# Recommendation model on one core: in the last step, the first half's second top layer placed behind the second half's Gram products

## The chip, the core and the metric

The kernel runs on one core of a Trainium2 chip. The metric is the device time of one execution in microseconds (us), the median of several runs. TensorE multiplies matrices, VectorE and ScalarE move and transform data, GpSimd issues the gathers of table rows, SyncE issues the plain transfers. In the profile they are called PE (PEld for its weight loads), DVE, ACT, POOL and SP.

## The reference

For 2048 samples the model runs a small net on 13 dense features, gathers 26 table rows of 64 numbers, forms all pairwise products of the 27 vectors, and runs a second net on them:

```
x = relu(dense @ Wb0 + bb0)            # 13 -> 512
x = relu(x @ Wb1 + bb1)                # -> 256
d = relu(x @ Wb2 + bb2)                # -> 64
sp = emb[arange(26)[None, :], sparse_idx]          # 2048 x 26 x 64, tables of 12500 rows
T = concatenate([sp, d[:, None, :]], axis=1)       # 27 vectors a sample
Z = einsum('bnd,bmd->bnm', T, T)                   # Gram products
h = concatenate([d, Z[:, lower triangle]], axis=1) # 64 + 351
h = relu(h @ Wt0 + bt0)                # -> 512
h = relu(h @ Wt1 + bt1)                # -> 256
p = sigmoid(h @ Wt2 + bt2)             # -> 1
```

## The kernel before, in words

The 2048 samples are taken in 8 steps of 256. A step gathers 52 pieces of 128 rows (26 tables, two halves of 128 samples), one indirect transfer each, issued by GpSimd (L260). All engines run their own programs, written out by hand in a fixed order, and wait for each other by semaphores; nothing is scheduled by a compiler. So the order on an engine is the order in which the code issues.

In the first seven steps TensorE works on the top net of the step before while rows of this step land. The last step (`last_step`, L477 for TensorE) is written differently: its gathers bring the first half's 26 pieces first, then the second half's, so that the first half can be finished while the second half still lands. For each half `h`:

- `turn_last(h, r)` (L334) transposes the rows of run `r` of tables (four tables a run, two in the last, r = 6) when they have landed; VectorE or ScalarE copies them out of PSUM (`spread_last`, L688 and L550).
- `gram_last(h)` (L373) forms the Gram products: 128 small matmuls, which the profile shows as 256 passes, since each f32 matmul of this kernel is two passes, a weight load and a matmul each. It waits for all copies of its half.
- VectorE transposes the products in two pieces (`turn_gram`, L693 and L695), ScalarE packs them (`pack`, L568), TensorE transposes three tiles (`turn_feat`, L383), ScalarE moves them (L574).
- `top_0` (L394 and L400) is the first top layer in four blocks of 128 outputs: a block is one matmul on the dense part (`top_0_d`) and three on the pairs. ScalarE and VectorE apply relu (L580, L701).
- the second top layer is one matmul that adds the bias (`top_1_bias`, L421) and four on the hidden layer (`top_1_sum`, L431). `top_1` is both in a row.
- `logit` (L706) is VectorE's product with the last weights; it reads the PSUM tile `ps_t1` of the second layer. The bias matmul of the second half waits for the first half's logit, since it overwrites that tile.

After the last logit come one sigmoid on ScalarE and the transfer of the result (L235). The code of the last step, of all three engines, is straight: no loop.

Of the kernel before, what the change touches and what calls it, by code (L numbers as in the profile page):

```python
# [91 lines left out]
def build(nc, x, idx, emb, wb0, bb0, wb1, bb1, wb2, bb2, wt0, wt1, bt1, wt2, bt2, out):  # L92
    emb_rows = emb.rearrange("t v d -> (t v) d")

    with ExitStack() as ctx:  # L95
# [100 lines left out]
        def top_0_blocks(u, side):  # L196


            if side == 0:
                return ps_t0[:, 0:2 * P].rearrange("p (m c) -> p m c", m=2)  # L200
            return ps_feat[u][:, 0:2, :]
# [10 lines left out]
        def unit_products(n):  # L212

            return ps_gram[:, :, 0:HALF * VECS].rearrange("p b (c v) -> p v b c", v=VECS)[:, 0:n]

        def turned_half(h, r):

            first, n = RUNS[r]
            part = slice(DIM * h, DIM * (h + 1))
            return (vecs_st[part, :, first:first + n].rearrange("p c t -> p t c"),  # L220
                    ps_turn[(h * NR + r) % 2][part, 0:n, :])
# [61 lines left out]
        def _(pe):  # L283
# [39 lines left out]
            def turn_last(h, r):  # L323

                first, n = RUNS[r]
                k = h * NR + r
                pe.wait_ge(rows_landed_last[h][r], 16 * n)
                if k >= 2 and k % 2 == 0:
                    pe.wait_ge(vecs_act, (STEPS - 1) * ACT_RUNS + k // 2)
                if k >= 2 and k % 2 == 1:  # L330
                    pe.wait_ge(vecs_dve, (STEPS - 1) * DVE_RUNS + k // 2)
                cols = DIM * (h + 1)
                for j in range(n):
                    turned = nc.tensor.transpose(ps_turn[k % 2][0:cols, j, :], rows[:, first + j, 0:cols], ident[:, :])  # L334
                turned.then_inc(rows_turned, 1)
# [21 lines left out]
            def gram_last(h):  # L357

                i = STEPS - 1

                pe.wait_ge(vecs_act, i * ACT_RUNS + (NR * (h + 1) + 1) // 2)
                pe.wait_ge(vecs_dve, i * DVE_RUNS + NR * (h + 1) // 2)
                if h == 0:
                    pe.wait_ge(d_placed, STEPS)
                else:

                    pe.wait_ge(gram_turned, i * 4 + 2)
                part = slice(DIM * h, DIM * (h + 1))
                for u in range(2):
                    for g in range(HALF):  # L370
                        for v in range(4):
                            c = 64 * u + 16 * v + g
                            summed = nc.tensor.matmul(  # L373
                                ps_gram[32 * v:32 * v + 32, u, g * VECS:(g + 1) * VECS],
                                vecs_st[part, c, :], vecs_st[part, c, 0:VECS],
                                start=True, stop=True, tile_position=(DIM * h, 32 * v))
                summed.then_inc(gram_summed, 1)

            def turn_feat(i, u):

                pe.wait_ge(feat_packed, i * 2 + u + 1)
                for k in range(PAIR_TILES):
                    turned = nc.tensor.transpose(ps_feat[u][0:PAIR_ROWS, k, :],  # L383
                                                 feat[:, u, k * PAIR_ROWS:(k + 1) * PAIR_ROWS], ident[:, :])
                turned.then_inc(feat_turned, 1)

            def top_0_d(i, u, m):

                if m == 0 and u == 0:
                    pe.wait_ge(d_copied, i + 1)  # L390
                if m == 0 and u == 1:

                    pe.wait_ge(t0_act, i * 2 + 1)
                nc.tensor.matmul(top_0_blocks(u, m // 2)[:, m % 2, :], wt0_sb[0:D_ROWS, PAIR_TILES, m * P:(m + 1) * P],  # L394
                                 d_t[:, u, :], start=True, stop=False)
# [10 lines left out]
            def top_0(i, u, blocks=range(T0 // P), begun=False):  # L406

                for m in blocks:
                    if m > 0 or not begun:
                        top_0_d(i, u, m)  # L410
                    if m == 0:

                        pe.wait_ge(feat_act, i * 2 + u + 1)
                    top_0_pairs(i, u, m)

            def top_1_bias(i, u):

                if u == 1:

                    pe.wait_ge(logit_ready, i * 2 + 1)  # L420
                nc.tensor.matmul(ps_t1[:, 0:T1], ones[0:1, :], bt1_sb[:, :], start=True, stop=False)  # L421

            def top_1_sum(i, u):

                for k in range(T0 // P):
                    if k == 0:

                        pe.wait_ge(t0_act, i * 2 + u + 1)
                    if k == 2:
                        pe.wait_ge(t0_dve, i * 2 + u + 1)  # L430
                    summed = nc.tensor.matmul(ps_t1[:, 0:T1], ht0_t[:, k, :], wt1_sb[:, k, :],  # L431
                                              start=False, stop=(k == T0 // P - 1))
                summed.then_inc(t1_summed, 1)
# [22 lines left out]
            def land(i, turn_run):  # L456

                turn_run(0)
                top_0(i - 1, 0)
                turn_run(1)  # L460
                turn_run(2)
                top_1(i - 1, 0)
                top_0(i - 1, 1)
                turn_run(3)
                turn_run(4)
                top_1(i - 1, 1)
                turn_run(5)
                turn_run(6)
# [8 lines left out]
            def last_step():  # L477
                i = STEPS - 1
                land(i, lambda r: turn_last(0, r))
                gram_last(0)  # L480
                turn_last(1, 0)
                turn_feat(i, 0)
                for r in range(1, NR - 3):
                    turn_last(1, r)

                top_0(i, 0, blocks=range(0, 2))
                turn_last(1, NR - 3)
                top_0(i, 0, blocks=range(2, 4))
                top_1_bias(i, 0)
                turn_last(1, NR - 2)  # L490
                top_1_sum(i, 0)
                turn_last(1, NR - 1)
                gram_last(1)

                top_0_d(i, 1, 0)
                top_1_bias(i, 1)
                turn_feat(i, 1)
                top_0(i, 1, begun=True)
                top_1_sum(i, 1)

            pe.wait_ge(bottom_loaded, 16 * BOTTOM_LOADS)
            bottom_0(0)
# [153 lines left out]
        def _(dve):  # L656
# [29 lines left out]
            def spread_last(h, r):  # L686
                dve.wait_ge(rows_turned, (STEPS + h) * NR + r + 1)
                nc.vector.tensor_copy(*turned_half(h, r)).then_inc(vecs_dve, 1)  # L688

            def turn_gram(i, u):  # L690

                dve.wait_ge(gram_summed, i * 2 + u + 1)
                nc.vector.transpose(gram_s[u][:, 0:VECS * SLOTS], unit_products(VECS)).then_inc(gram_turned, 1)  # L693

                nc.vector.transpose(gram_s[u][:, VECS * SLOTS:WRAP * SLOTS], unit_products(DELTAS))\  # L695
                    .then_inc(gram_turned, 1)

            def relu_top(i, u):

                dve.wait_ge(t0_summed, i * 4 + 2 * u + 2)  # L700
                nc.vector.tensor_scalar(ht0_t[:, 2:4, :], top_0_blocks(u, 1), 0.0, None, ALU.max).then_inc(t0_dve, 1)  # L701

            def logit(i, u):

                dve.wait_ge(t1_summed, i * 2 + u + 1)
                nc.vector.scalar_tensor_tensor(out=ht1_w[:, :], in0=ps_t1[:, 0:T1], scalar=0.0, in1=wt2_sb[:, :],  # L706
                                               op0=ALU.max, op1=ALU.mult,
                                               accum_out=logits[:, bass.ds(i * 2 + u, 1)]).then_inc(logit_ready, 1)
# [4 lines left out]
            def land(i, spread_run, head=None):  # L713
                spread_run(1)
                relu_top(i - 1, 0)
                logit(i - 1, 0)
                spread_run(3)
                if head:
                    head()
                relu_top(i - 1, 1)  # L720
                logit(i - 1, 1)
                spread_run(5)
# [18 lines left out]
            def last_step():  # L741
                i = STEPS - 1
                land(i, lambda r: spread_last(0, r))
                turn_gram(i, 0)
                spread_last(1, 0)
                spread_last(1, 2)
                spread_last(1, 4)
                relu_top(i, 0)
                spread_last(1, 6)
                logit(i, 0)  # L750
                turn_gram(i, 1)
                relu_top(i, 1)
                logit(i, 1)

# [79 lines left out]
```

## Time and profile before

| | |
|---|---|
| time, median of 3 runs | 552.0 us (551.23 to 552.62) |
| span of the profiled execution, first to last instruction | 551.0 us |
| TensorE busy (matmul) | 310.5 us, 56% |
| GpSimd busy | 394.4 us, 72% |
| VectorE, ScalarE busy | 127.8 us and 134.6 us |
| mean granted TensorE clock | 0.703 of full speed |

The profiled execution has no time of its own beside its span; the span is 1.0 us below the median of the runs. The chain of waits, followed back from the last instruction, names at each point what the end depended on. A timeline row gives the start, the busy time, the engine, the line, what is written and read, the count, and in brackets the idle time ahead and what ended it. A windows row gives for a stretch the busy time of each engine with its instructions, and the granted clock, where 1.00 is 2.4 GHz and 0.50 is 1.2 GHz.

### The profile page before, as it was taken

The numbers are of one execution on the slowest core, as the hardware profiler recorded it, in microseconds if no ns is written. First come the engines' busy times: TensorE is split into PE (matmuls) and PEld (weight loads), VectorE is DVE, ScalarE is ACT, GpSimd is POOL, SyncE is SP. The second block draws the span as 40 slices with busy tenths as digits, with TensorE's granted clock in tenths as the row PEclk, the third lists the DMA queues.
The fourth block names the chain that finished last, engine by engine and source line by source line (L and its number), as shares of the span: only waits on it lengthen the run. The fifth ranks groups of instructions, "written<-read, shape, count | busy, mean of one in ns | idle before, by whom it ended". The sixth has DMA issues, their size and how long they took to land.

```text
span 551.0 us, 8032 instructions
## 1 busy us (share of the span) xinstructions
PE 310.5 (56%) x3370; PEld 226.6 (41%) x3370; DVE 127.8 (23%) x190; ACT 134.6 (24%) x197; POOL 394.4 (72%) x422
## 2 busy tenths in 40 slices
PE   4799966825556327164373455552463742775566
PEld 1333325713445217152272334441253522664546
DVE  5213232222220222220212202302222112221110
ACT  1124333502242213122152021420133221311101
POOL 5777777777777777777777777777777777777710
PEclk9996796776586566675576765766667756795686
DMA  7233323333243322333233332343323432333310
GB/s 204 25 27 28 26 27 28 28 26 27 29 26 27 26 27 26 27 26 26 26 26 26 26 27 26 27 26 27 28 25 26 26 26 27 26 27 28 28 10 2
DMA packets 16181, 16.53 MB, mean 30 GB/s; under 512 B 7691, under 2 KB 8972, under 8 KB 16153
## 3 DMA queue, kind: packets, MB, share of 16 engines
q0 software_dynamic: 13312, 13.66, 31.7%
q1 hardware_dynamic: 2170, 2.41, 1.4%
q10 hardware_dynamic: 684, 0.24, 0.2%
q8 instruction: 12, 0.20, 0.1%
q14 instruction: 3, 0.02, 0.0%
HBM read 16.28 MB, written 0.01 MB: 30 GB/s over the span
## 4 chain that ended last, share of the span: by engine, by line
POOL 68%; issue 24%; PE 4%; DMA 2%; DVE 1%; POOLq 1%; ACT 1%; DVEq 0%; ACTq 0%
POOL rows L260 68%; DMA rows<-in_emb,idx_step 1%; PE ps_t L431 1%; DMA idx_raw<-in_idx 1%; PE ps_gram L351 1%; PE ps_t L400 1%; PE ps_gram L373 0%; PE ps_feat L400 0%; PE ps_turn L334 0%; ACT vecs_mv L545 0%; POOLq L95 0%; DVE gram_s L693 0%; DVE gram_s L695 0%; PE ps_feat L383 0%; PE ps_feat L394 0%
## 5 line engine op out<-in xcount | busy, mean ns | idle before, releaser
L260 POOL DMA_INDIRECT rows<-in_emb,idx_step x416 | 392.7, 944 | 130.8 <-issue 130.5
L320 PE MATMUL ps_turn<-ident,rows 128*128 128x128 f32 x182 | 41.0, 365 | 167.3 <-DMA rows<-in_emb,idx_step 162.1
L320 PEld LDWEIGHTS ps_turn<-ident,rows 128*128 128x128 f32 x182 | 26.2, 181 | 183.6 <-issue 174.3
L545 ACT ACTIVATE vecs_st<-ps_turn 128x512 f32<-128x512 f32 (+1 forms) x28 | 25.9, 926 | 215.2 <-PE ps_turn L320 215.0
L351 PE MATMUL ps_gram<-vecs_mv,vecs_st 128*32 128x54 f32 x1792 | 43.5, 296 | 25.2 <-ACT vecs_mv L545 13.3
L545 ACT ACTIVATE vecs_mv<-ps_turn 64x512 f32<-64x512 f32 (+1 forms) x56 | 54.0, 964 | 0.3
L351 PEld LDWEIGHTS ps_gram<-vecs_mv,vecs_st 128*32 128x32 f32 x1792 | 40.8, 173 | 29.3 <-issue 13.8
L431 PE MATMUL ps_t<-wt_sb,ht_t 128*128 128x256 f32 x128 | 52.0, 578 | 0.0
L683 DVE COPY vecs_st<-ps_turn 128x512 f32<-128x512 f32 x21 | 21.3, 1014 | 120.5 <-PE ps_turn L320 120.5
L683 DVE COPY vecs_mv<-ps_turn 64x512 f32<-64x512 f32 x42 | 43.7, 1042 | 0.3
L431 PEld LDWEIGHTS ps_t<-wt_sb,ht_t 128*128 128x128 f32 x128 | 36.4, 298 | 15.4 <-issue 8.2
L706 DVE SCALAR_TENSOR_TENSOR ht_w<-ps_t,wt_sb 128x256 f32<-128x256 f32 x16 | 6.8, 424 | 136.6 <-PE ps_t L431 136.6
L693 DVE STREAM_TRANSPOSE gram_s<-ps_gram 128x864 f32<-128x864 f32 x16 | 17.3, 1083 | 82.1 <-PE ps_gram L351 67.7
L400 PE MATMUL ps_t<-feat_t,wt_sb 117*128 117x128 f32 x192 | 34.3, 328 | 0.6 <-ACT feat_t L574 0.6
L297 PE MATMUL ps_t<-hb,wb_sb 128*128 128x512 f32 x64 | 31.7, 653 | 3.3 <-DVE hb L668 3.3
L400 PEld LDWEIGHTS ps_t<-feat_t,wt_sb 117*128 117x128 f32 x192 | 31.2, 240 | 0.9 <-ACT feat_t L574 0.9
L400 PE MATMUL ps_feat<-feat_t,wt_sb 117*128 117x128 f32 x192 | 29.7, 296 | 0.0
L400 PEld LDWEIGHTS ps_feat<-feat_t,wt_sb 117*128 117x128 f32 x192 | 27.4, 215 | 0.0
L568 ACT ACTIVATE feat<-gram_s 128x351 f32<-128x351 f32 x16 | 13.4, 840 | 56.0 <-DVE gram_s L695 56.0
L297 PEld LDWEIGHTS ps_t<-hb,wb_sb 128*128 128x128 f32 x64 | 13.4, 216 | 21.1 <-issue 16.3
L383 PE MATMUL ps_feat<-ident,feat 128*117 128x128 f32 x48 | 12.5, 383 | 14.5 <-ACT feat L568 14.5
L421 PE MATMUL ps_t<-bt_sb,ones 1*128 1x256 f32 x32 | 17.3, 637 | 0.0
(52 smaller groups left out, 235.8 us busy)
## 6 DMA issues: line engine op xcount, KB each, us to landing
rows<-in_emb,idx_step POOLq DMA_INDIRECT x416, 3.4
wt_sb<-in_wt SPq DMA_DIRECT2D x1, 1024.0 KB
wb_sb<-in_wb SPq DMA_DIRECT2D x1, 512.0 KB
wt_sb<-in_wt SPq DMA_DIRECT2D x1, 512.0 KB
idx_raw<-in_idx SPq DMA_DIRECT2D x1, 208.0 KB, 3.9
wt_sb<-in_wt ACTq DMA_DIRECT2D x1, 128.0 KB
x_t<-in_x ACTq DMA_DIRECT2D x1, 104.0 KB
wb_sb<-in_wb SPq DMA_DIRECT2D x1, 64.0 KB
```

The source lines that it names most:

```text
L260: nc.gpsimd.indirect_dma_start(rows[:, t, h * DIM:(h + 1) * DIM], None, emb_rows, bass.IndirectOffsetOnAxis(idx_step[:, c:c + 1], 0)).then ...
L297: summed = nc.tensor.matmul((ps_t0, ps_t1)[m][:, :], wb1_sb[:, k, m * P:(m + 1) * P], hb0[:, k, :], start=(k == 0), stop=(k == B0 // P - 1))
L320: turned = nc.tensor.transpose(ps_turn[r % 2][:, j, :], rows[:, first + j, :], ident[:, :])
L351: summed = nc.tensor.matmul(ps_gram[32 * v:32 * v + 32, b, g * 2 * VECS:(g + 1) * 2 * VECS], vecs_st[:, c, :], vecs_mv[:, c, :, :].rearran ...
L383: turned = nc.tensor.transpose(ps_feat[u][0:PAIR_ROWS, k, :], feat[:, u, k * PAIR_ROWS:(k + 1) * PAIR_ROWS], ident[:, :])
L400: summed = nc.tensor.matmul(top_0_blocks(u, m // 2)[:, m % 2, :], wt0_sb[0:PAIR_ROWS, k, m * P:(m + 1) * P], feat_t[:, u, k, :], start=Fal ...
L421: nc.tensor.matmul(ps_t1[:, 0:T1], ones[0:1, :], bt1_sb[:, :], start=True, stop=False)
L431: summed = nc.tensor.matmul(ps_t1[:, 0:T1], ht0_t[:, k, :], wt1_sb[:, k, :], start=False, stop=(k == T0 // P - 1))
L545: moved = nc.scalar.activation(to, source, ACT.Copy)
L568: nc.scalar.activation(feat[:, u, :].rearrange("p (e i) -> p e i", e=DELTAS), bass.AP(gram_s[u], SLOTS, [[WRAP * SLOTS, P], [SLOTS, DELTAS ...
L683: moved = nc.vector.tensor_copy(to, source)
L693: nc.vector.transpose(gram_s[u][:, 0:VECS * SLOTS], unit_products(VECS)).then_inc(gram_turned, 1)
```

## The change

On TensorE the bias matmul and the four summing matmuls of the first half's second top layer no longer stand around the transposes of run 5 of the second half, but behind all of the second half's Gram products and ahead of `top_0_d` of the second half. The second half's bias matmul moves from ahead of `turn_feat` to directly ahead of its sum, since both layers are now issued by the unsplit `top_1`. On VectorE the first half's logit moves behind the two transposes of the second half's Gram products. The number of instructions is the same, and ScalarE, GpSimd and SyncE issue what they issued.

```diff
@@ -486,17 +486,15 @@
                 top_0(i, 0, blocks=range(0, 2))
                 turn_last(1, NR - 3)
                 top_0(i, 0, blocks=range(2, 4))
-                top_1_bias(i, 0)
                 turn_last(1, NR - 2)
-                top_1_sum(i, 0)
                 turn_last(1, NR - 1)
                 gram_last(1)
 
+                top_1(i, 0)
                 top_0_d(i, 1, 0)
-                top_1_bias(i, 1)
                 turn_feat(i, 1)
                 top_0(i, 1, begun=True)
-                top_1_sum(i, 1)
+                top_1(i, 1)
 
@@ -747,8 +745,8 @@
                 spread_last(1, 4)
                 relu_top(i, 0)
                 spread_last(1, 6)
+                turn_gram(i, 1)
                 logit(i, 0)
-                turn_gram(i, 1)
                 relu_top(i, 1)
                 logit(i, 1)
```

TensorE before, from the last block of the first half's `top_0` to the second half's `top_0_d` (`ps_turn` takes transposed rows, `ps_gram` Gram products, `ps_t` the top layers):

```order
L421 MATMUL ps_t<-bt_sb,ones 128x256
L334 MATMUL ps_turn<-ident,rows 128x128 [waits vecs_act,rows_landed_last1_5]
L334 MATMUL ps_turn<-ident,rows 128x128 x3
L431 MATMUL ps_t<-wt_sb,ht_t 128x256 [waits t0_act]
L431 MATMUL ps_t<-wt_sb,ht_t 128x256
L431 MATMUL ps_t<-wt_sb,ht_t 128x256 [waits t0_dve]
L431 MATMUL ps_t<-wt_sb,ht_t 128x256
L334 MATMUL ps_turn<-ident,rows 128x128 [waits vecs_dve,rows_landed_last1_6]
L334 MATMUL ps_turn<-ident,rows 128x128
L373 MATMUL ps_gram<-vecs_st 32x27 [waits gram_turned,vecs_dve,vecs_act]
L373 MATMUL ps_gram<-vecs_st 32x27 x127
L394 MATMUL ps_t<-d_t,wt_sb 128x128 [waits t0_act]
```

TensorE now, the same stretch:

```order
L334 MATMUL ps_turn<-ident,rows 128x128 [waits vecs_act,rows_landed_last1_5]
L334 MATMUL ps_turn<-ident,rows 128x128 x3
L334 MATMUL ps_turn<-ident,rows 128x128 [waits vecs_dve,rows_landed_last1_6]
L334 MATMUL ps_turn<-ident,rows 128x128
L373 MATMUL ps_gram<-vecs_st 32x27 [waits gram_turned,vecs_dve,vecs_act]
L373 MATMUL ps_gram<-vecs_st 32x27 x127
L421 MATMUL ps_t<-bt_sb,ones 128x256
L431 MATMUL ps_t<-wt_sb,ht_t 128x256 [waits t0_act]
L431 MATMUL ps_t<-wt_sb,ht_t 128x256
L431 MATMUL ps_t<-wt_sb,ht_t 128x256 [waits t0_dve]
L431 MATMUL ps_t<-wt_sb,ht_t 128x256
L394 MATMUL ps_t<-d_t,wt_sb 128x128 [waits t0_act]
```

Five matmuls, ten passes, left the space between the landing rows and now follow the Gram products. VectorE before, at the end of its program (`ht_w` is written by the logit, `gram_s` takes the transposed products):

```order
L688 COPY vecs_st<-ps_turn 64x2x128 [waits rows_turned]
L706 SCALAR_TENSOR_TENSOR ht_w,logits<-ps_t,wt_sb 128x256 [waits t1_summed]
L693 STREAM_TRANSPOSE gram_s<-ps_gram 128x864 [waits gram_summed]
L695 STREAM_TRANSPOSE gram_s<-ps_gram 128x416
L701 TENSOR_SCALAR ht_t<-ps_feat 128x256 [waits t0_summed]
L706 SCALAR_TENSOR_TENSOR ht_w,logits<-ps_t,wt_sb 128x256 [waits t1_summed]
```

VectorE now, the same place (the changed kernel is two lines shorter above it, so its line numbers are lower by two):

```order
L686 COPY vecs_st<-ps_turn 64x2x128 [waits rows_turned]
L691 STREAM_TRANSPOSE gram_s<-ps_gram 128x864 [waits gram_summed]
L693 STREAM_TRANSPOSE gram_s<-ps_gram 128x416
L704 SCALAR_TENSOR_TENSOR ht_w,logits<-ps_t,wt_sb 128x256 [waits t1_summed]
L699 TENSOR_SCALAR ht_t<-ps_feat 128x256 [waits t0_summed]
L704 SCALAR_TENSOR_TENSOR ht_w,logits<-ps_t,wt_sb 128x256 [waits t1_summed]
```

The first logit and the two transposes have changed places; nothing else moved on VectorE.

## Rows read from the trace of the kernel before

**Rows 1.** The page: span, and the chain by engine.

```profile
span 551.0 us, 8032 instructions
...
POOL 68%; issue 24%; PE 4%; DMA 2%; DVE 1%; POOLq 1%; ACT 1%; DVEq 0%; ACTq 0%
```

**Rows 2.** The chain's end in order of time: start us, us, what.

```profile
522.43 3.35 DMA rows<-in_emb,idx_step
...
532.45 2.37 issue
...
548.36 0.42 DVE ht_w L706
```

**Rows 3.** Timeline of GpSimd: the last gather.

```profile
524.93 0.95 POOL L260 DMA_INDIRECT rows<-in_emb,idx_step  x1 [0.30 <-issue]
```

**Rows 4.** Timeline of TensorE's matmuls, from 526 us to the end.

```profile
526.65 3.24 PE L431 MATMUL ps_t<-wt_sb,ht_t 128*128 128x256 f32 x8
529.72 0.38 PE L334 MATMUL ps_turn<-ident,rows 128*128 128x128 f32 x2
530.83 1.62 PE L373 MATMUL ps_gram<-vecs_st 64*32 64x27 f32 x170 [0.73 <-issue]
534.82 0.93 PE L373 MATMUL ps_gram<-vecs_st 64*32 64x27 f32 x86 [2.37 <-issue]
535.68 0.49 PE L394 MATMUL ps_t<-d_t,wt_sb 65*128 65x128 f32 x2
536.10 1.16 PE L421 MATMUL ps_t<-bt_sb,ones 1*128 1x256 f32 x2
538.29 0.99 PE L383 MATMUL ps_feat<-ident,feat 128*117 128x128 f32 x3 [1.03 <-ACT feat L568]
539.86 1.65 PE L400 MATMUL ps_t<-feat_t,wt_sb 117*128 117x128 f32 x6 [0.58 <-ACT feat_t L574]
...
546.42 1.91 PE L431 MATMUL ps_t<-wt_sb,ht_t 128*128 128x256 f32 x8
```

**Rows 5.** Timeline of VectorE around the first half's logit.

```profile
530.14 0.59 DVE L688 COPY vecs_st<-ps_turn 64x256 f32<-64x256 f32 x1 [6.47 <-PE ps_turn L334]
530.76 0.42 DVE L706 SCALAR_TENSOR_TENSOR ht_w<-ps_t,wt_sb 128x256 f32<-128x256 f32 x1
```

**Rows 6.** Windows: us, busy us (instructions) by engine, PEclk, DMA share, GB/s.

```profile
525.95:529.30 3.35, 3.35 (x11) 2.81 (x12) 0.00 (x0) 1.03 (x1) 0.00 (x0) 0.50 0.16 10
529.40:532.70 3.30, 2.33 (x175) 1.91 (x173) 1.02 (x3) 0.00 (x0) 0.00 (x0) 1.00 0.02 5
532.80:536.10 3.30, 1.28 (x89) 1.13 (x89) 0.30 (x1) 0.00 (x0) 0.00 (x0) 1.00 0.02 5
536.20:539.50 3.30, 2.05 (x5) 1.02 (x5) 1.18 (x2) 1.01 (x2) 0.00 (x0) 0.50 0.00 0
...
543.00:546.40 3.40, 3.40 (x17) 3.40 (x17) 0.00 (x0) 0.38 (x1) 0.00 (x0) 0.50 0.02 5
546.50:549.00 2.50, 1.82 (x9) 1.25 (x8) 0.85 (x3) 0.13 (x1) 0.00 (x0) 1.00 0.00 0
```

**Rows 7.** Timeline of TensorE's matmuls from 486 to 505 us.

```profile
486.24 0.39 PE L394 MATMUL ps_feat<-d_t,wt_sb 65*128 65x128 f32 x2
...
487.13 0.39 PE L394 MATMUL ps_feat<-d_t,wt_sb 65*128 65x128 f32 x2
...
489.62 1.99 PE L431 MATMUL ps_t<-wt_sb,ht_t 128*128 128x256 f32 x8
...
495.81 0.64 PE L334 MATMUL ps_turn<-ident,rows 128*64 128x128 f32 x2 [1.89 <-DMA rows<-in_emb,idx_step]
497.12 1.85 PE L373 MATMUL ps_gram<-vecs_st 64*32 64x27 f32 x117 [0.68 <-ACT vecs_st L550]
500.36 2.14 PE L373 MATMUL ps_gram<-vecs_st 64*32 64x27 f32 x128 [1.39 <-issue]
504.37 0.41 PE L373 MATMUL ps_gram<-vecs_st 64*32 64x27 f32 x11 [1.87 <-issue]
```

**Rows 8.** Windows of an earlier stretch, columns as in rows 6.

```profile
488.50:492.00 3.50, 3.11 (x16) 2.02 (x13) 1.62 (x3) 1.33 (x3) 2.66 (x3) 1.00 0.34 26
496.50:505.00 8.50, 4.63 (x258) 4.28 (x259) 0.18 (x1) 0.57 (x1) 6.37 (x8) 0.50 0.31 31
```

## The prediction

> **What bounds the kernel.** I read the chain by engine first: GpSimd holds 68% of it, with gathers issued one after another [rows 1]. The change touches nothing ahead of 523 us, so only the end counts. The chain's end shows where GpSimd hands over: a gather begun at 522.43 lands 3.35 us later [rows 2], and the last one begins at 524.93 [rows 3]. From there TensorE's timeline is nearly the whole chain: the first half's second layer (526.65), the transposes of run 6 (529.72), the Gram products (530.83, resumed at 534.82), the turning of the pair features (538.29), the first top layer (539.86), the second (546.42) [rows 4]. Then the windows are read for the clock: half speed from 525.95, full from 529.4 to 536.1, half from 536.2 to 546.4, full at the end [rows 6]. So an edit here has three prices: its passes, the wait it hides in, and what it does to the clock.
>
> **Step 1, the Gram products start earlier.** The last gather, at the same 3.35 us, lands at 524.93 + 3.35 = 528.28. Run 6 was turned only at 529.72, because the eight passes at 526.65 stood ahead of it on TensorE. Without them it starts at 528.3. From that turn to the first Gram pass it took 1.11 us (530.83 - 529.72), in which VectorE's 0.59 us copy lies [rows 5]. A turn after an idle TensorE costs 0.64 us instead of 0.38 [rows 7, 4], so 1.11 to 1.37 us. The Gram products begin at 529.4 to 529.7: 1.2 us earlier. The ends: where the eight passes run at full speed (1.99 us, [rows 7, 8]) they would be over by about 528.5 before too, and the gain is 0.2; at most it is 1.4. The bias matmul ahead of run 5 lay in a wait for rows and was free. The first logit began at 530.76 [rows 5], after the copy and beside the Gram products: moving it gains nothing.
>
> **Step 2, the Gram products themselves.** Before they took 530.83 to 535.75, 4.9 us, with a pause of 2.37 us after 170 passes in which TensorE waits for nothing shown [rows 2, 4]. The first half's Gram products pause as well, after 117 and after 245 passes, that is 128 apart [rows 7]: the pause goes by the position in the instruction stream. Ten passes fewer stand ahead now, so I expect it after 180 passes instead of 170, with 76 behind it. In full clock nothing changes in the sum: passes ahead and behind add up to 256 as before, 4.9 us. In half clock a pass takes 2.14/128 = 16.7 ns, and from one resumption to the next, 128 passes and a pause, 504.37 - 500.36 = 4.0 us [rows 7]. Counting 52 passes, one such stretch, and 76 passes: 0.9 + 4.0 + 1.3 = 6.2 us, 1.2 more. Which clock? Before, the full speed at 529.4 came after a stretch of 3.35 us with TensorE busy in all of it [rows 6], and the eight passes were most of that. They are gone; from about 526.9 to 528.3 TensorE now idles. I take half speed, +1.2 us (bounds 0 and 1.3). That cancels step 1: the products end at about 535.75, as before.
>
> The Trainium skill, "Runtime: NRT & Kernel Launch", section "Instruction fetch mechanics", says that instructions come in blocks of 256 and that the cost of crossing a block is mostly hidden. The count agrees with the 128 passes of two instructions between pauses; "mostly hidden" does not, at 1.39, 1.87 and 2.37 us [rows 7, 4]. By that rule the Gram products would take 2.4 us less before and after alike, and the difference would stay.
>
> **Step 3, the moved layer where it now stands.** From the last Gram pass (535.75) to the turning of the features (538.29) there are 2.5 us, VectorE's transposes and ScalarE's packing, in which TensorE had only the dense part and the second half's bias. Now stand there, with 0.4 us for the dense part (535.68 to 536.10) and the first layer's ten passes: at half clock 3.1 us for eight (526.65 to 529.72) and 0.8 for the bias at the same price a pass, together 4.3 us, 1.8 more than the cover; at full clock 1.8 to 1.9 for eight (546.42), 0.5 and 0.2, together 2.6, 0.1 more [rows 4, 7]. Behind it wait `turn_feat` and with it ScalarE's move and all of `top_0`. The clock rises somewhere in this run, I think near its end: +1.3 us (bounds 0.1 and 1.8). The logit on VectorE then comes at about 540, seven microseconds before its next customer: free.
>
> **Step 4, the first top layer of the second half.** Its 30 passes took 539.86 to 546.42, 6.6 us, at half clock [rows 4, 6]. In full clock a block of eight takes 487.13 - 486.24 = 0.89 us [rows 7], so 30 take 3.3. Before, TensorE had idled ahead of it, and the clock rose only 6.6 us into the unbroken run. The rise at 529.4 came about 3.5 us into one that began at 525.82. Now TensorE is in unbroken work from the resumed Gram products, near 534.5, to about 540; with 3.5 to 6.6 us the rise falls at 538.0 to 541.1. Then comes about 1 us of waiting for ScalarE's move. Once up, the clock held through windows with 2.33 and 1.28 of 3.30 us busy and fell after the second [rows 6]; so it probably holds for a good part of `top_0`. I take two thirds of it in full clock: -2.1 us (bounds 0 and -3.3).
>
> The Trainium skill, "TensorE: Matmul & The Clock Gate", section "What's actually happening", says the monitor is free-running and does not start with the kernel. No row here shows the phase of another execution; by that rule step 4 differs from run to run, and the two medians carry some of it.
>
> **Step 5, the second layer of the second half.** Its bias, free before in the wait at 536.10, now stands at the end of the path: two passes, at full clock 1.91/8 x 2 = 0.45 us (0.8 at half). If the clock has fallen by then, the sum costs 3.1 instead of 1.9: up to +1.6 together. I take +0.4. What follows the last pass, from logit to end (548.36 to 551.0), stays.
>
> **Sum**, in the profiled execution: -1.2 + 1.2 + 1.3 - 2.1 + 0.4 = -0.4 us on 551.0. I round to -0.3, as step 1 is at the upper side of its bounds; the median of the runs stands 1.0 us above the span, so 552.0 - 0.3 = 551.7 us.
>
> **Rivals.**
> - *The clock is up for all of `top_0`.* TensorE no longer idles between Gram products and features, so the rise comes inside the moved layer and holds. Then step 4 is -3.3: -1.2 + 1.2 + 1.3 - 3.3 + 0.4 = -1.6, 550.4 us. For it: the rise 3.5 us into the run at 525.82. Against it: the 6.6 us run before 546.4. The Trainium skill's "TensorE: Matmul & The Clock Gate", section "Why this matters for your kernels", advises continuous work for this reason; the trace agrees in direction (busy 3.35 of 3.35, then 1.00), not in a sure moment. Chance 0.22.
> - *Also the Gram products keep full clock*, since the layer's first part on TensorE and the blocks before it suffice. Step 2 is then 0: -2.8, 549.2 us. Against it: the clock had fallen at 525.95 even before. Chance 0.08.
> - *Slower: the layer in front of the features is paid in full and nothing comes back.* Place: the 2.5 us between last Gram pass and `turn_feat`. If the clock rises only after `turn_feat` has been held back and `top_0` runs at half again: -1.2 + 1.2 + 1.8 + 0 + 0.4 = +2.2, 554.2 us; with the rise in the last third of `top_0` +1.1, 553.1. It decides from the point where the rise comes later than 541. Chance 0.15, a good half of it beyond +0.3%.
> - *Nothing to see:* run 6 lands later than the 3.35 us say and the eight passes cost no start, and the layer runs in full clock in its cover: -0.2 + 0 + 0.1 + 0 + 0.4 = +0.3, 552.3 us. Chance 0.10.
>
> **How the numbers follow.** My forecast has 0.45, with its own range from 551.0 to 552.8. A change under 0.3%, 1.65 us, is about what a measurement of this kernel cannot tell from none. Faster by more: 0.08 from the second rival and 0.05 from the first one's edge, 0.13. Slower by more: 0.08. The same: 0.79. The range takes in the first rival and the mild form of the slower one: 550.2 to 553.0.
>
> **What the profile of the changed kernel would show.** Step 1: run 6 turned at 528.3 to 528.5 after a wait for rows, no L431 group before it. Step 2: the pause after 180 passes, and about 1.2 us more for the whole at clock 0.50. Step 3: the features' turn starts right behind the dense part, later than 2.5 us after the last Gram pass, with ScalarE's packing long done. Step 4: `top_0` shorter than 6.6 us, and the windows over it at 1.00 in part. Step 5: L421 directly ahead of the last L431. I am wrong if the Gram products run at full clock, if the features' turn still waits for ScalarE, or if the clock stays at half through `top_0`.

## The result and the profile after

The changed kernel takes 552.05 us (median of 20 runs, 551.28 to 554.01), the kernel before 551.33 us in the same comparison (20 runs, 550.02 to 552.62). The ratio is 1.0023, 95% interval 1.0014 to 1.0031. The medians lie 0.7 us apart and the means, which the ratio follows, 1.2 us; 0.3 us faster was forecast. The time is inside the range and the change is within 0.3%, but the sign is wrong.

The profiled execution of the changed kernel has a span of 552.3 us; its own time is 554.01, the span plus 1.7. With the same 1.7 the profiled execution of before (551.0) would be a run of 552.7, at the top of its 20 runs, not 1.0 us below a median. Both traces are of executions at the upper end of their kernel's times. For the changed kernel that end is a group of its own: four of its 20 runs, the profiled one among them, took 553.87 to 554.01 us at a mean granted clock of 0.697 to 0.700, the other sixteen 551.28 to 552.66 us at 0.702 to 0.712.

The page's chain by engine gives GpSimd, issue, TensorE and DMA the same shares as before (68%, 24%, 4%, 2%). The chain's end of the changed kernel (start us, us, what):

```profile
524.87 3.38 DMA rows<-in_emb,idx_step
528.25 0.04 issue
528.29 0.69 PE ps_turn L334 x2
528.99 0.73 issue
529.71 2.66 PE ps_gram L373 x180
532.37 1.43 issue
533.80 1.27 PE ps_gram L373 x76
535.07 1.15 PE ps_t L421 x2
536.22 3.71 PE ps_t L431 x8
539.93 0.43 PE ps_t L394 x2
540.35 0.65 PE ps_feat L383 x3
```

Against [rows 2 to 4]: the transposes of run 6 are now released by the DMA of the last gather, where before they followed the second layer on TensorE, and that layer stands in the chain between the Gram products and the features. VectorE's transposes and ScalarE's packing are no longer in the chain. The timeline of the engines around that place:

```profile
536.73 0.83 ACT L566 ACTIVATE feat<-gram_s 128x351 f32<-128x351 f32 x1 [9.28 <-DVE gram_s L693]
...
540.15 0.85 PE L383 MATMUL ps_feat<-ident,feat 128*117 128x128 f32 x3
...
541.57 1.65 PE L400 MATMUL ps_t<-feat_t,wt_sb 117*128 117x128 f32 x6 [0.58 <-ACT feat_t L572]
...
546.92 0.69 PE L421 MATMUL ps_t<-bt_sb,ones 1*128 1x256 f32 x2
...
547.54 1.99 PE L431 MATMUL ps_t<-wt_sb,ht_t 128*128 128x256 f32 x8
...
549.57 0.42 DVE L704 SCALAR_TENSOR_TENSOR ht_w<-ps_t,wt_sb 128x256 f32<-128x256 f32 x1 [2.12 <-PE ps_t L431]
```

The packed features are ready at 537.56 and are turned at 540.15, 2.6 us later and without an idle bracket: TensorE was busy. The windows of the changed kernel, to be laid beside [rows 6]:

```profile
528.40:531.70 3.30, 2.57 (x151) 2.20 (x155) 0.59 (x1) 0.00 (x0) 0.00 (x0) 0.50 0.02 5
531.80:535.10 3.30, 1.87 (x117) 1.69 (x108) 0.00 (x0) 0.00 (x0) 0.00 (x0) 0.50 0.02 5
535.20:538.50 3.30, 3.30 (x8) 2.20 (x9) 1.50 (x2) 0.83 (x1) 0.00 (x0) 0.50 0.00 0
538.60:541.90 3.30, 2.72 (x10) 2.14 (x9) 0.43 (x2) 0.49 (x1) 0.00 (x0) 0.50 0.00 0
542.00:545.30 3.30, 3.30 (x17) 3.30 (x17) 0.00 (x0) 0.34 (x1) 0.00 (x0) 0.50 0.03 5
545.50:549.00 3.50, 3.50 (x23) 2.89 (x22) 0.42 (x1) 0.00 (x0) 0.00 (x0) 1.00 0.00 0
```

The clock (second last but one column) is at half through the Gram products, the moved layer and more than half of `top_0`, and rises at 545.4. The difference of the two traces by places:

| place | before | after | difference |
|---|---|---|---|
| first Gram pass | 530.83 | 529.71 | -1.1 |
| Gram products, first to last pass | 4.9 | 5.4 | +0.4 |
| last Gram pass to the turn of the features | 2.5 | 5.1 | +2.5 |
| turn to `top_0` | 1.6 | 1.4 | -0.1 |
| `top_0` from its pair matmuls | 6.6 | 5.35 | -1.2 |
| last layer up to the logit | 1.9 | 2.65 | +0.7 |

Together +1.2, the difference of the spans (551.04 and 552.25 us, not rounded).

### The profile page after: what moved, and what is told of

The parts are those of the page before. It is cut to its first block, busy times and chain, and to the rows that moved or that the text cites. A ratio compares the mean times of both kernels' runs of the same rounds, so it can differ in the third digit from the quotient of the medians.

```text
span 552.3 us, 8032 instructions
## 1 busy us (share of the span) xinstructions
PE 315.5 (57%) x3370; PEld 232.9 (42%) x3370; DVE 127.6 (23%) x190; ACT 134.6 (24%) x197; POOL 394.4 (71%) x422
## 4 chain that ended last, share of the span: by engine, by line
POOL 68%; issue 24%; PE 4%; DMA 2%; POOLq 1%; ACT 0%; DVE 0%; DVEq 0%; ACTq 0%
POOL rows L260 68%; DMA rows<-in_emb,idx_step 1%; PE ps_t L431 1%; PE ps_gram L373 1%; DMA idx_raw<-in_idx 1%; PE ps_gram L351 1%; PE ps_t L400 1%; PE ps_t L421 0%; PE ps_feat L400 0%; ACT vecs_mv L543 0%; POOLq L95 0%; PE ps_t L394 0%; POOLq L254 0%; PE ps_turn L320 0%; PE ps_turn L334 0%
## 5 line engine op out<-in xcount | busy, mean ns | idle before, releaser
L543 ACT ACTIVATE vecs_st<-ps_turn 128x512 f32<-128x512 f32 (+1 forms) x28 | 25.9, 926 | 208.9 <-PE ps_turn L320 208.9
L351 PE MATMUL ps_gram<-vecs_mv,vecs_st 128*32 128x54 f32 x1792 | 42.6, 290 | 26.6 <-ACT vecs_mv L543 13.3
L431 PE MATMUL ps_t<-wt_sb,ht_t 128*128 128x256 f32 x128 | 53.9, 594 | 0.0
L351 PEld LDWEIGHTS ps_gram<-vecs_mv,vecs_st 128*32 128x32 f32 x1792 | 39.8, 168 | 30.7 <-issue 15.4
L400 PE MATMUL ps_t<-feat_t,wt_sb 117*128 117x128 f32 x192 | 40.0, 368 | 0.6 <-ACT feat_t L572 0.6
L400 PEld LDWEIGHTS ps_t<-feat_t,wt_sb 117*128 117x128 f32 x192 | 37.4, 283 | 0.9 <-ACT feat_t L572 0.9
L400 PE MATMUL ps_feat<-feat_t,wt_sb 117*128 117x128 f32 x192 | 27.6, 281 | 0.0
L400 PEld LDWEIGHTS ps_feat<-feat_t,wt_sb 117*128 117x128 f32 x192 | 25.3, 200 | 0.0
L383 PE MATMUL ps_feat<-ident,feat 128*117 128x128 f32 x48 | 11.2, 350 | 15.4 <-ACT feat L566 15.4
L334 PE MATMUL ps_turn<-ident,rows 128*64 128x128 f32 (+1 forms) x52 | 10.8, 348 | 14.3 <-DMA rows<-in_emb,idx_step 14.0
```

Of the source, the lines that this page charges most:

```text
L351: summed = nc.tensor.matmul(ps_gram[32 * v:32 * v + 32, b, g * 2 * VECS:(g + 1) * 2 * VECS], vecs_st[:, c, :], vecs_mv[:, c, :, :].rearran ...
L400: summed = nc.tensor.matmul(top_0_blocks(u, m // 2)[:, m % 2, :], wt0_sb[0:PAIR_ROWS, k, m * P:(m + 1) * P], feat_t[:, u, k, :], start=Fal ...
L543: moved = nc.scalar.activation(to, source, ACT.Copy)
```

## The experiments

Theory 1 is that the moved layer overruns its cover, the 2.5 us between the last Gram pass and the turn of the features; rival 2 is the clock in the Gram products; rival 3 is VectorE's order. The tail is what follows the last Gram pass, unless another start is named.

**What the base was.** In the first three comparisons the kernel before itself took 842.8, 836.9 and 836.6 us, in the fourth 835.6, and in the fifth 551.6 again, on a chip that had given 836.9. The extra time is TensorE's: in e1's waits,

```profile
PE ps_gram L351 <- issue: 323.4, 276, 2.7
```

(waiter, what ended the wait; us in total, times, longest), where the page of the kernel before has 25.2 us of idle time in all ahead of these passes. In these runs GpSimd's gathers of the last step are over before TensorE asks for the last rows, so run 6 never waits. A ratio there prices the change where it has no wait for rows to fill; what transfers is the tail in the traces, the straight code of the last step. The full changed kernel was not run in these series, so no run there can be compared with it, and of the full kernel before no trace was kept there.

**e1, e5: the first half's bias ahead of run 5 again.**

```diff
                 top_0(i, 0, blocks=range(2, 4))
+                top_1_bias(i, 0)
                 turn_last(1, NR - 2)
...
-                top_1(i, 0)
+                top_1_sum(i, 0)
                 top_0_d(i, 1, 0)
```

> The changed kernel, but with the first half's bias matmul back in the wait for rows ahead of run 5; only its four summing matmuls stay behind the Gram products. Theory 1 (the moved layer overruns the 2.5 us between the last Gram pass and the turn of the features): in the changed kernel the bias took 535.00 to 536.14, 1.1 us at half clock, all of it on the path; so 0.6 to 1.1 us less than the changed kernel, which is 0.3 slower to 0.4 us faster than the kernel before. Rival 2 (the loss comes from the clock in the Gram products, since the eight summing passes no longer stand ahead of them): the same time as the changed kernel, +0.7 us against before. Rival 3 (VectorE's order costs): the same, +0.7 us.

> The same edit as e1, hoping for a chip on which the kernel is bound by the gathers as in its profile: the first half's bias matmul back ahead of run 5. Theory 1 (the moved layer overruns the cover): 0.6 to 1.1 us less than the changed kernel, against before -0.4 to +0.3 us. Rival 2 (clock in the Gram products): +0.7 us against before, as the changed kernel.

Measured: ratio 0.999 (0.9967 to 1.0013) and 0.9967 (0.9951 to 0.9983). The second is 2.8 us faster than before, more than the 0.4 us that was expected at most, so the ratio does not test the theory. In e5's trace the last Gram pass ends at 822.10, the eight passes run 822.03 to 825.60 and the features are turned at 826.03: 3.9 us (3.9 in e1 too), between 2.5 and the changed kernel's 5.1. Without the bias the delay is 1.2 us less, near the 1.1 us that the bias takes in the changed kernel's trace, as theory 1 has it, and the sum alone still overruns. Eight passes cost 3.6 us at half clock.

**e2, e6: the second half's bias behind the turn of the features.**

```diff
                 turn_feat(i, 1)
+                top_1_bias(i, 1)
                 top_0(i, 1, begun=True)
-                top_1(i, 1)
+                top_1_sum(i, 1)
```

> The changed kernel, but with the second half's bias matmul directly behind the turn of the features, where TensorE waits about 0.6 to 1.0 us for ScalarE's move, instead of at the end of the path. Theory 1 with its second term (this bias costs 546.92 to 547.54, 0.6 us, at the end): 0.5 us less than the changed kernel, about +0.2 us against before. If that bias was hidden or the chain ends elsewhere: +0.7 us as in the changed kernel. Rivals 2 and 3: +0.7 us.

> The same edit as e2: the second half's bias matmul behind the turn of the features. Theory 1 with its second term (0.6 us at the end of the path): +0.2 us against before. If the term is hidden anyway: +0.7 us.

Measured: 0.999 (0.997 to 1.0009) and 0.9967 (0.995 to 0.9984). In e6's trace this bias runs 822.19 to 822.84, `top_0` begins at 822.84, 1.1 us after the features' turn (821.76; 1.4 in the changed kernel), and the last sum follows `top_0` at once. From the start of the last layer to the span's end it is 4.6 us, where e5 with the bias at the end has 5.3. The term of the late bias is real; the ratio is again far from what was expected (+0.2 us) and can't tell it from e5.

**e3: VectorE's order alone, and s4, the same in the shortened form below.**

```diff
-                logit(i, 0)
                 turn_gram(i, 1)
+                logit(i, 0)
```

> The kernel before with only VectorE's part of the change: the first logit behind the transposes of the second half's Gram products. Theory 1: no difference, within 0.1 us, since the second half's bias, which waits for this logit, still ends ahead of the features (logit at 537.4 to 537.9, features at 538.3), or a few tenths slower where the late bias (0.6 to 1.1 us) now runs past 538.3 and holds the features back: 0 to +0.7 us. Rival 3 (VectorE's order alone is the loss): +0.7 us with ScalarE or VectorE later and the bias on time.

Measured for e3: 1.0016 (0.9997 to 1.0035), which decides nothing. Its trace does show where the order costs:

```profile
831.42 0.83 ACT L568 ACTIVATE feat<-gram_s 128x351 f32<-128x351 f32 x1 [7.71 <-DVE gram_s L695]
...
831.77 1.22 PE L421 MATMUL ps_t<-bt_sb,ones 1*128 1x256 f32 x2 [1.59 <-DVE ht_w L706]
...
832.91 0.99 PE L383 MATMUL ps_feat<-ident,feat 128*117 128x128 f32 x3
```

The second half's bias waits for the delayed logit, and the features, packed at 832.25, are turned at 832.91, 3.2 us after the last Gram pass.

**e4, e7: one matmul behind the Gram products.** `top_1(i, 0)` becomes a single matmul, the last of the four summing ones; the bias and three terms are left out.

> The changed kernel, but the first half's second top layer behind the Gram products is one matmul (two passes) instead of bias and four: the bias and three of the four terms are left out. Theory 1: it fits into the 2.5 us, the features are turned on time, so 1.5 to 2.5 us less than the changed kernel at an unchanged clock; where the shorter work also leaves the clock lower in the first top layer, 1 us of that goes back. Against before: -0.3 to -1.5 us. Rival 2 (clock in the Gram products): as the changed kernel, +0.7 us, or slower since less work keeps the clock up.

> The same edit as e4: behind the Gram products one matmul instead of five; the bias and three of the four terms of the first half's second layer are left out. Theory 1: features turned about 2.5 us after the last Gram pass; -0.3 to -1.5 us against before. Rival 2: +0.7 us or more.

Measured: 0.9985 (0.9965 to 1.0005) and 0.9964 (0.9944 to 0.9984). The features are on time (815.53 to 818.08 in e7, 2.6 us), but `top_0` takes 5.6 us instead of 3.5 in e5, since the clock rises 8.5 us after the end of the products instead of 4.9. Both ratios are no better than those of e5 and e6, and e7's 3.0 us below before is again more than was expected.

**e8: a spare layer added to the kernel before.**

```diff
...
                 gram_last(1)
 
+                top_1_spare()
                 top_0_d(i, 1, 0)
                 top_1_bias(i, 1)
```

`top_1_spare` is the bias and four matmuls into a PSUM tile that nobody reads.

> The kernel before, unchanged in every place, plus a spare copy of the first half's second layer (bias and four matmuls, into a PSUM tile that nobody reads) behind the second half's Gram products. It adds only what stands in the cover. Theory 1: the ten passes took 4.7 us in the changed kernel and the cover is 2.5 us with 1.6 us of other work in it, so +2 to +3.2 us against before at an unchanged clock, less 1 to 2 us where the unbroken work raises the clock for the first top layer: +0.5 to +2.5. Rival 2 (the loss is the clock in the Gram products, the layer itself is hidden): 0 to +0.3 us, or below 0.

Measured: 1.0026 (1.0007 to 1.0045), +2.2 us of 836.9. The edit adds nothing but the layer in the cover, and the Gram products stay as they were, so ten passes there are not free and rival 2 does not explain this loss. Its trace:

```profile
821.35 0.93 PE L373 MATMUL ps_gram<-vecs_st 64*32 64x27 f32 x86 [1.82 <-issue]
...
827.25 0.59 PE L383 MATMUL ps_feat<-ident,feat 128*117 128x128 f32 x3
```

The features are turned 5.0 us after the last Gram pass (822.28). But the clock rises at 826.0 and the whole tail is 14.2 us, less than the 15.3 of the kernel before in its own trace and the 15.6 of e3, which has the same order without the layer. So one trace does not show where the 2.2 us of the runs arise.

**s1 to s4: the last step alone, in a short form.** Three steps of the eight are left, and the second half's gathers, from the fourth piece on, are held until the first half is turned. s1 is the order of before, s2 the whole change, s3 is s2 with e5's edit, s4 is s1 with e3's edit.

> A shortened form of the kernel before, made to see the last step alone: 3 steps instead of 8 (the samples of the other five are left out, their outputs are not computed), and GpSimd holds the second half's gathers from the fourth piece on until TensorE has turned the first half's last run, so that they land at about the distance from it that the full kernel's trace shows (29 us from 495.8 to the last gather at 524.9). It is the base of s2 to s4. Expected: its last step looks as in the trace of the kernel before, run 6 behind the eight passes, Gram products 4.9 us, features 2.5 us behind them.

> The same shortened form with the whole change. Theory 1 (the moved layer overruns the cover by more than the earlier start gives): 0.4 to 1.2 us more than s1, as in the full kernels (+0.72 us). If the full kernels' difference was something of the steps ahead: no difference.

> s2 with the first half's bias matmul back ahead of run 5, in the wait for rows. Theory 1: 0.6 to 1.1 us less than s2. Rival 2 (the loss is the clock in the Gram products): as s2.

> s1 with only VectorE's part of the change (the first logit behind the transposes of the Gram products). Theory 1: as s1, or up to 0.4 us more, since the second half's bias waits for this logit and stands ahead of the features. Rival 3 (VectorE's order is the loss): +0.7 us.

The medians, 335.24, 334.22, 333.39 and 335.95 us, have five or six runs each and ranges of 3 to 6 us. s2 was expected 0.4 to 1.2 us above s1 and lies 1.0 us below it, s3 lies 0.8 us below s2 as expected and s4 0.7 us above s1; all of this is inside that spread. Rows were early again, so s1 is not the case of the trace. The traces can be read. From the start of run 3's transposes to the end they are 28.3, 25.9, 26.2 and 30.3 us. s2 is 2.4 us shorter than s1 here, not longer: this pair, with its rows early, does not repeat the loss. In s4 the features come late for the reason seen in e3, not by theory 1:

```profile
319.81 0.39 DVE L709 SCALAR_TENSOR_TENSOR ht_w<-ps_t,wt_sb 128x256 f32<-128x256 f32 x1
...
320.27 1.22 PE L424 MATMUL ps_t<-bt_sb,ones 1*128 1x256 f32 x2 [1.27 <-DVE ht_w L709]
321.42 0.99 PE L386 MATMUL ps_feat<-ident,feat 128*117 128x128 f32 x3
```

The second half's bias waits for the delayed logit and holds the features from 320.8 to 321.4. So VectorE's edit alone makes the features 0.6 us late there; the whole change has moved that bias and does not pay it.

**t1 to t4: rows signalled instead of gathered.** Three steps, and the rows are a constant. GpSimd only raises the rows' semaphores; `iota` instructions set the time of runs 5 and 6. t1 is the order of before, t2 the whole change, t3 is t2 with e7's edit.

> A form of the kernel before for the last step alone: 3 steps instead of 8, and no gathers (the rows are a constant, so the outputs are not the model's). GpSimd signals the rows instead; in the last step it signals run 5 after three timed instructions of 1.2 us from the end of run 4's transposes, and run 6 after two more, which is where the rows landed in the full kernel's trace (4.4 us and 2.5 us). Base of t2 to t4. Expected: the tail from run 5 to the end as in the trace of before, 25.2 us from 525.8 to 551.0, run 6 behind the eight passes.

> The same form with the whole change. Theory 1: 0.4 to 1.2 us more than t1, as in the full kernels; run 6 turned about 1 us earlier after a wait, features turned 4 to 5 us after the last Gram pass instead of 2.5. If the full difference came from elsewhere: within 0.2 us of t1.

> t2 with the moved layer cut to one matmul (the bias and three of four terms are left out). Theory 1: features on time, 2.5 us after the last Gram pass, and 1 to 2.5 us less than t2, so below t1 by about 0.5 us or more. Rival 2 (clock in the Gram products; less work before them than in t1): as t2 or slower.

> t2 with the same work split: both bias matmuls ahead of run 5 in the wait for rows (the second half's into another PSUM tile, so that it does not wait for the first logit), two of the four summing matmuls behind the Gram products, two behind the turn of the features in the wait for ScalarE's move. Theory 1: each part fits its wait, within 0.5 us; 1.5 to 2.5 us less than t2 and 0.7 to 1.5 us less than t1. If the loss is not the overrun: as t2.

The split of t4, against the changed kernel:

```diff
...
+                top_1_bias(i, 0)
+                pe.wait_ge(t0_dve, i * 2 + 1)
+                nc.tensor.matmul(ps_last, ones[0:1, :], bt1_sb[:, :], start=True, stop=False)
                 turn_last(1, NR - 2)
...
-                top_1(i, 0)
+                top_1_part(i, 0, ps_t1[:, 0:T1], range(0, 2))
                 top_0_d(i, 1, 0)
                 turn_feat(i, 1)
+                top_1_part(i, 0, ps_t1[:, 0:T1], range(2, 4))
                 top_0(i, 1, begun=True)
-                top_1(i, 1)
+                top_1_part(i, 1, ps_last, range(0, 4))
```

The second half's layer is summed into `ps_last`, another PSUM tile, and its logit reads that one.

An `iota` took 0.52 us, not 1.2, so run 6 followed run 5 by 1.3 us in t2 and not by 2.5: my timing was wrong. The medians are 185.84, 188.60, 187.01 and 187.31 us over the runs taken, five or six each; t1 has one run of 270.56 us among them. Differences stand already ahead of the tail (run 4 is turned at 156.4, 159.8, 159.4 and 160.9 us), so again the traces decide. From run 5's transposes to the end they give 23.0, 23.1, 22.6 and 19.5 us: t2 is not the expected 0.4 to 1.2 us above t1, and t4 gains more than expected, since runs 5 and 6 had both come when it turned run 5.

**u1, u2: t2 and t4 with the timing mended.**

> The form of t2 (whole change, 3 steps, rows signalled and not gathered) with eight timed instructions ahead of run 5 and four ahead of run 6, 4.4 us and 2.5 us. Theory 1: from the start of run 5's transposes to the span's end 26.0 to 26.8 us, as in the full changed kernel's trace (525.73 to 552.3, 26.6) and above the 25.2 us of the kernel before; features turned 4 to 5 us after the last Gram pass. If the tail is 25.2 us or less: the full difference came from the clock's phase.

> The form of t4 (both biases ahead of run 5, two summing matmuls behind the Gram products, two behind the turn of the features), arrival as in u1. Theory 1: from run 5's transposes to the end 1.5 to 2.5 us less than u1, 24.0 to 25.0 us. If the overrun is not the loss: as u1.

Medians 191.75 and 188.80 us, six runs each; their ratios to the kernel before, 0.3446 (0.3433 to 0.3460) and 0.3413 (0.3400 to 0.3426), lie 1.8 us apart. The execution in u1's trace took 192.6 us, 0.85 above its median, that in u2's 188.54. From run 5's transposes to the end it is 24.0 and 21.7 us. The 2.3 us less is as expected. The 24.0 is not the expected 26.0 to 26.8: the clock rose at 180.5, right before the features, and `top_0` ran at full speed throughout. It is also below the 25.2 us under which I had expected the full kernels' difference to be one of the clock's phase. So u1 shows the features late, by 4.7 us against the 4 to 5 expected, and it shows that the longer tail of the changed kernel's trace, 26.6 us against 25.2, is no fixed price of the change: with an earlier rise of the clock the same order took 24.0. u1's rows:

```profile
176.16 1.22 PE L434 MATMUL ps_t<-bt_sb,ones 1*128 1x256 f32 x2
...
177.30 3.55 PE L444 MATMUL ps_t<-wt_sb,ht_t 128*128 128x256 f32 x8
...
180.91 0.49 PE L396 MATMUL ps_feat<-ident,feat 128*117 128x128 f32 x3
```

and u2's:

```profile
174.09 2.07 PE L460 MATMUL ps_t<-wt_sb,ht_t 128*128 128x256 f32 x4
...
175.96 0.63 PE L409 MATMUL ps_t<-d_t,wt_sb 65*128 65x128 f32 x2
...
176.71 0.99 PE L398 MATMUL ps_feat<-ident,feat 128*117 128x128 f32 x3
177.49 1.52 PE L460 MATMUL ps_t<-wt_sb,ht_t 128*128 128x256 f32 x4
...
178.85 0.83 PE L415 MATMUL ps_t<-feat_t,wt_sb 117*128 117x128 f32 x6
```

Two matmuls and the dense part fit into the cover; two more stand in ScalarE's move and overrun it a little, since the step from the turn to `top_0` takes 2.1 us instead of 1.6 before. Against u1 the tail is 2.0 us shorter: the features are turned 2.1 us earlier, the step to `top_0` is 1.1 us longer, `top_0` 0.2 us shorter, and 0.7 us come from the second half's bias, which no longer stands at the end. The split thus moves two things, and 0.7 us of its gain is not the overrun. The windows of u1 over the moved layer and over `top_0`:

```profile
176.30:180.40 4.10, 4.10 (x9) 2.87 (x10) 1.57 (x2) 0.83 (x1) 0.00 (x0) 0.50 0.00 0
180.60:185.50 4.90, 4.32 (x37) 4.00 (x35) 0.43 (x2) 0.88 (x2) 0.00 (x0) 1.00 0.00 0
```

**The tails side by side**, in us, from one trace each:

| | last Gram pass to features' turn | from there to the span's end | sum |
|---|---|---|---|
| full kernels, before / after | 2.5 / 5.1 | 12.8 / 12.1 | 15.3 / 17.2 |
| s1 / s2 | 2.5 / 4.2 | 11.3 / 10.0 | 13.8 / 14.2 |
| s3 (bias early) / s4 (VectorE's order alone) | 3.1 / 3.2 | 10.0 / 12.8 | 13.1 / 15.9 |
| t1 / t2 | 2.5 / 5.1 | 12.6 / 10.3 | 15.1 / 15.4 |
| t3 (one matmul) / t4 (split) | 2.6 / 2.5 | 12.6 / 10.2 | 15.1 / 12.8 |
| u1 / u2 (split) | 4.7 / 2.6 | 10.0 / 10.1 | 14.6 / 12.6 |

The first column is theory 1: the whole layer makes the features late by 1.7 to 2.5 us in all four traces here that have it (2.5 in e2, e6 and e8 too), without its bias by 0.6 (1.4 in e1 and e5), one matmul or the split by nothing; s4's 0.6 us is the late bias. The second column is the clock, and 0.7 us of the late bias. The order of before gives 11.3 or 12.6 to 12.8, by where the rise falls in `top_0`; the whole layer gives 10.0 to 10.3 three times and 12.1 once. One matmul is on time and gets nothing back from the clock: in sum it is no better than the whole layer. The split has both, 12.6 to 12.8.

So the delay of the features is shown with the layer there and with it taken out. The sign of the whole change is not settled by these tails. The mean sum is 14.7 us in the three traces with the order of before and 15.3 in the four with the change, the Gram products take 4.9 and 5.2 us in the mean, and the start came 1.1 us earlier: together -0.2 us, with single sums of one order up to 3.0 us apart.

## Why the prediction was wrong

**Step 1** was right. Run 6 was turned at 528.29 after a wait for rows, the Gram products began 1.1 us earlier (forecast 1.2). A detail was misread: the turn of 0.64 us against 0.38 is not the price of an idle TensorE but of the clock, which stood at 0.50 at 495.8 [rows 7]; run 6 took 0.69 us at 0.50 here.

**Step 2**: the place was right and the size too large. The pause came after 180 passes, the clock was at 0.50, but the products took 5.4 us, not 6.2. The pause was 1.43 us where I had counted 1.87 from the first half, and the 180 passes ahead of it took 2.66 us, 14.8 ns each and not 16.7. The pause is shorter where the passes ahead of it are slow: 1.35 and 1.73 us in u2 and u1, which ran them at 0.50 as well, and 1.8 to 2.6 us in the traces that ran all or most of them at full clock. Why it is so was not tested. +0.4 instead of +1.2. So the earlier start was kept in part, and this term is in the kernel's favour.

**Step 3 is the step that failed**: "together 4.3 us, 1.8 more than the cover", taken as +1.3 "since the clock rises somewhere in this run". Measured +2.5. The layer and the dense part took 535.00 to 540.15, 5.15 us in place of 4.3, and the features came 2.5 us late. The clock did not rise in it, in the trace after; in u1 it rose right at its end and the delay was 2.1 us, in s2 0.4 us ahead of the features and it was 1.7. And the price at half clock was too low: I read it from 526.65 to 529.72 as 3.1 us, but the clock had risen at 529.4, inside that stretch [rows 6]. The eight passes cost 3.6 us at half clock (536.14 to 539.72, the same in e5), the bias 1.1 instead of 0.8. With +2.5 in place of +1.3 the forecast's own sum is +0.8 us and has the right sign.

**Step 4** had the mechanism right and compared it with the wrong execution. In the trace before `top_0` took 6.6 us because the clock rose only behind it, at 546.4; s1, in the same order, has the rise in its middle:

```profile
322.40:325.80 3.40, 3.37 (x16) 3.37 (x17) 0.00 (x0) 0.00 (x0) 0.00 (x0) 0.50 0.00 0
326.00:329.40 3.40, 3.40 (x23) 2.85 (x22) 0.42 (x1) 0.20 (x1) 0.00 (x0) 1.00 0.00 0
```

and takes 5.1. I credited the change with -2.1 against 6.6; the trace after gives -1.2, and against 5.1 a fully clocked `top_0` (3.55 in s2, t2 and u1) is only -1.5. The full kernels could fit this: a changed execution with a fully clocked `top_0` would be 552.3 - 1.8 = 550.5 us long, which is near its median less 1.7 (550.35), and the execution of before with s1's `top_0` would be 549.5, near its 549.6. The sum for these two is -1.1 + 0.4 + 2.5 - 0.1 - 1.5 + 0.7 = +0.9, beside the measured +0.7 (medians) and +1.2 (means). For the changed kernel its separate group of four slower runs speaks for it. For the kernel before it is a guess: s1 is the only one of five traces with this order of `top_0` that took 5.1 us; t1, s4 and e3 took 6.4, 6.6 and 6.3. Against 6.6 a full clock would be worth 3.0 us and the sum would be -0.6. Which of them the median execution of before is like stays open; only the two executions at the upper end have a trace of the full kernels. The Trainium skill, "TensorE: Matmul & The Clock Gate", section "What's actually happening", has the monitor free-running. The three traces in the order of before agree, with the rise at different places of `top_0` and 5.1 to 6.6 us for it. I had named this and still used one execution as the base.

**Step 5**: +0.7 instead of +0.4. The bias costs 0.6 us at full clock, since the sum behind it starts 0.62 us later, and its two passes are no cheaper for having one row (1.15 us at half clock). The forecast's price was low, and its working has a slip: 1.91/8 x 2 is 0.48, not 0.45. From the start of the last layer to the end it is 5.3 us in every trace with the bias there and 4.6 in every one without.

**The rivals.** The clock up for all of `top_0` came true in three of the four traces with the whole change, though not in that of the full kernel. Gram products at full clock did not, in the full kernel. The slower rival named the right place and had 0.15; of the stories told it came nearest, with +2.2 or +1.1 us. "Nothing to see" had the nearest time, 552.3 us, by luck: its mechanism is refuted by 528.29. That 552.05 lies so near the 551.7 of the forecast is luck too, since the base of 552.0 from three runs stands 0.7 us above the 551.33 of twenty. Rival 3 of the experiments is not the loss, and rival 2 has 0.4 us of it.

Open is the full kernel with the split layer: it was not run. With -2.3 us in u2 against u1, 0.7 of it from the bias at the end, and +0.7 us of the change it should lie near 549.8 us, an estimate from these numbers.

## What to carry to other kernels

Before moving work into a wait, add up at the slower clock all that will stand there, and take each price from a stretch that lies wholly at one clock. Compare the profiled execution's time with the median of the runs before any of its stretches is taken as the base of a gain: where the clock moves between executions, the base must be a range. Work that is too large for one wait can be cut at its matmuls over two; in t4 and u2 the features came on time so, and `top_0` still ran in 3.35 us at full clock.

## What the runs showed that was not expected

The same kernel took 551.6 us in one comparison and 836.9 us in another on the same chip. In the long executions TensorE issued Gram passes in groups of one to six, 0.7 us and more apart, while GpSimd was gathering; in s1's timeline of the last step (weight loads left out):

```profile
291.48 0.95 POOL L261 DMA_INDIRECT rows<-in_emb,idx_step  x1 [0.30 <-issue]
292.07 0.20 PE L376 MATMUL ps_gram<-vecs_st 64*32 64x27 f32 x1 [1.90 <-issue]
293.46 0.20 PE L376 MATMUL ps_gram<-vecs_st 64*32 64x27 f32 x1 [1.20 <-issue]
294.87 0.20 PE L376 MATMUL ps_gram<-vecs_st 64*32 64x27 f32 x1 [1.20 <-issue]
296.27 2.03 PE L376 MATMUL ps_gram<-vecs_st 64*32 64x27 f32 x132 [1.20 <-issue]
```

The last gather is issued at 291.48, and from 296.27 132 passes run in 2.03 us. What brings this about stays open; no run tried to change it, and in other executions the gathers run and TensorE does not stall so.
